# One layer of RWKV attention and a mixture of experts: all 36 expert pairs moved behind the last chunk, with the reciprocal in PSUM and eight late buffers

## The reference, cut to what matters

```python
x = x + attn(layernorm(x))      # 16 sequences of 256 tokens
x = x + moe(layernorm(x))       # 8 experts, top 2
# attn:
xn = ln(x); xp = shift(xn)
k, v = mix(xn, xp) @ Wk, mix(xn, xp) @ Wv;  r = sigmoid(mix(xn, xp) @ Wr)
a = ew * a + exp(k) * v;  b = ew * b + exp(k)      # a scan over the tokens
x = x + r * (a / (b + 1e-8)) @ Wo
yn = ln(x); kk = relu((0.5 * yn + 0.5 * shift(yn)) @ Wfk) ** 2
x = x + sigmoid(yn @ Wfr) * (kk @ Wfv)
# moe: scores = x @ gate.T; the 2 best experts of each token, softmax over the 2
y = sum of prob * ((silu(h1) * h2) @ w3[e]),  h1, h2 = x @ w12[e]
```

## Time and profile before

| what | value |
|---|---|
| median of 3 runs | 342.45 us |
| the profiled execution, its own time | 343.89 us |
| its span, first to last instruction | 342.2 us |
| PE busy | 267.1 us (78%) |
| DVE busy | 250.8 us (73%) |
| POOL busy | 213.2 us (62%) |
| ACT busy | 196.7 us (57%) |
| mean granted clock of TensorE, 1 being full | 0.902 |

### The profile page before, as it was taken

How to read it: one execution, slowest core, us unless ns; L and a number is a source line. 1 busy time by engine, 2 the same in 40 slices (tenths; PEclk the granted TensorE clock), 3 DMA queues, 4 the chain that set the end, 5 groups by cost and what they waited for, 6 DMA issues and landing times.

```text
span 342.2 us, 6282 instructions
## 1 busy us (share of the span) xinstructions
PE 267.1 (78%) x1684; PEld 210.0 (61%) x1684; DVE 250.8 (73%) x767; ACT 196.7 (57%) x412; POOL 213.2 (62%) x225
## 2 busy tenths in 40 slices
PE   0588599998969699794798799547999999989500
PEld 0234266665737357472587699436998999989400
DVE  3089998999799797999948657684466565565773
ACT  2546578887758738483496385323566665665100
POOL 5223457357857768578377775777777565665770
PEclk9999899999989969897699899856999999999855
DMA  7920000000101101011253111141522232232876
GB/s 265 445 66 1 0 0 33 1 34 23 40 31 42 54 23 41 32 42 54 65 129 106 39 51 61 39 118 49 131 72 82 79 92 81 81 83 73 269 262 228
DMA packets 22418, 29.23 MB, mean 85 GB/s; under 512 B 4317, under 2 KB 15583, under 8 KB 22128
## 3 DMA queue, kind: packets, MB, share of 16 engines
q1 hardware_dynamic: 14832, 13.45, 13.9%
q0 software_dynamic: 4352, 8.47, 7.4%
q10 hardware_dynamic: 3200, 6.90, 5.4%
HBM read 15.09 MB, written 12.14 MB: 80 GB/s over the span
## 4 chain that ended last, share of the span: by engine, by line
DVE 37%; PE 19%; issue 12%; POOL 9%; DMA 8%; ACT 2%; SPq 1%; DVEq 0%; POOLq 0%; ACTq 0%
PE p_up L831 10%; DVE rw L959 4%; DVE st L891 4%; DMA xg<-rows_d 3%; POOL res_d L449 3%; DMA res_d<-yo,xg 3%; DVE rden L952 3%; DVE gate_h L1121 2%; DVE num L946 2%; DVE den L942 2%; PE p_up L738 2%; PE p_f L750 2%; DVE xm L996 2%; POOL rows_d L431 2%; DVE mv L898 2%
## 5 line engine op out<-in xcount | busy, mean ns | idle before, releaser
L431 POOL DMA_INDIRECT rows_d<-rows,pos x64 | 66.4, 1037 | 23.6 <-issue 23.3
L831 PE MATMUL p_up<-xgT,w_up 128*128 128x128 f32 x576 | 74.4, 285 | 2.8 <-DVE hid L1125 2.8
L831 PEld LDWEIGHTS p_up<-xgT,w_up 128*128 128x128 f32 x576 | 71.3, 202 | 4.0 <-issue 3.4
L449 POOL DMA_INDIRECT res_d<-yo,xg x48 | 47.6, 991 | 26.2 <-issue 15.2
L1121 DVE SCALAR_TENSOR_TENSOR gate_h<-th,p_up 128x512 f32<-128x512 f32 x36 | 24.7, 687 | 41.5 <-ACT th L606 40.1
L626 ACT ACTIVATE w_up<-w_exp 128x512 f32 x72 | 41.4, 622 | 6.9 <-DVE slot_w L1105 4.6
L606 ACT ACTIVATE th<-p_up 128x512 f32<-128x512 f32 x36 | 21.4, 596 | 40.8 <-PE p_up L831 35.4
L738 PE MATMUL p_up<-ysum,w_sb 128*128 128x512 f32 x64 | 36.6, 675 | 2.9 <-POOL ysum L410 2.5
L750 PEld LDWEIGHTS p_f<-wfv_half,kk 128*128 128x128 f32 x256 | 31.1, 192 | 4.4 <-issue 3.5
L750 PE MATMUL p_f<-wfv_half,kk 128*128 128x128 f32 x256 | 32.7, 277 | 0.0
L449 POOL DMA_INDIRECT res_d<-o_raw x24 | 23.4, 974 | 9.9 <-issue 6.6
(11 more groups left out here) (169 smaller groups left out, 559.0 us busy)
## 6 DMA issues: line engine op xcount, KB each, us to landing
o_raw<-res_d SPq DMA_DIRECT2D x16, 256.0 KB, 5.2
xg<-rows_d SPq DMA_DIRECT2D x48, 65.0 KB, 2.0
w_exp<-experts ACTq DMA_DIRECT2D x1, 3072.0 KB, 16.8
x_all<-x SPq DMA_DIRECT2D x10, 256.0 KB, 2.3
out<-x_all ACTq DMA_DIRECT2D x8, 256.0 KB, 2.4
o_raw<-rows_d SPq DMA_DIRECT2D x24, 65.0 KB, 2.0
x_all<-x SPq DMA_DIRECT2D x1, 1536.0 KB, 16.6
rows_d<-rows,pos POOLq DMA_INDIRECT x64, 2.4
```

Source lines behind the costliest of these rows:

```text
L431: pool.indirect_dma_start(out=rows_d[:, :], out_offset=bass.IndirectOffsetOnAxis(ap=row, axis=0), in_=rows_of[is_last(c)][:, t, k, :], in_ ...
L449: pool.indirect_dma_start(out=res_d[:, :], out_offset=bass.IndirectOffsetOnAxis(ap=row, axis=0), in_=yo[b][:, n, :], in_offset=None, bound ...
L831: mm = pe.matmul(p_up[b][:, n, h * P:(h + 1) * P], w_up[q % 2][:, n, h * P:(h + 1) * P], xgT[q % 2][:, n, :], start=True, stop=True)
```

## The change

- No pair is woven into the pipeline on any engine. All 36 stand in `rest` behind the last chunk, alternate between the two bank pairs of PSUM from the first on, and the guards that kept woven pairs and chunks apart are empty. `early_shares`, five small DVE instructions, moves to iteration 10.
- `rden` is no tile of SBUF any more. It is the bank of `p_v`. So `v_in(c)` waits for `rw` of chunk c - 1 (it waited for `ekv` of that chunk), and `invert` waits for `ekv`.
- The rows and positions of even and odd chunks have a buffer each; chunk c waits for chunk c - 2.
- The late pairs have 8 buffers in 3 rounds (there were 6 in 4).
- Two early pairs share a semaphore for their loads.

```diff
-BUFS = 6
+BUFS = 8
-LAST_SINGLE = 6
+LAST_SINGLE = 0
-        rden = sb("rden", [P, CT]); gated = sb("gated", [P, CT]); rw = sb("rw", [P, CT])
+        gated = sb("gated", [P, CT]); rw = sb("rw", [P, CT])
+        rden = p_up[1][:, 1, :]
-            if c <= EARLY_CHUNKS:
-                after(eng, "dispatched_early", 16 * TPC * TOPK * c)
-            elif not is_last(c):
-                after(eng, "dispatched", 16 * TPC * TOPK * (c - EARLY_CHUNKS))
+            if c >= 2:
+                eng.wait_ge(dispatch_sem(c - 2), 16 * TPC * TOPK * ((c - 2) % EARLY_CHUNKS // 2 + 1))
-                loaded = S[f"early_loaded{q}" if q < EARLY_PAIRS else f"xg_loaded{b}"]
+                loaded = S[f"early_loaded{q // 2}" if q < EARLY_PAIRS else f"xg_loaded{b}"]
-                        row = pos_of[is_last(c)][:, k, t:t + 1]
+                        row = pos_of[c % 2][:, k, t:t + 1]
-            v_in = project(1, p_v, "v_done", lambda c: [("ekv_ready", c)])
+            v_in = project(1, p_v, "v_done", lambda c: [("rw_ready", c)])
 # invert
                 after(dve, "den_eps", c + 1)
+                after(dve, "ekv_ready", c + 1)
                 dve.reciprocal(rden[:, :], den[:, :]).then_inc(S["rden_ready"], 1)
 # up, pair 0
-                    pe.wait_ge(S["ekv_ready"], CHUNKS)
+                    pe.wait_ge(S["rw_ready"], CHUNKS)
 # POOL: the woven scatters of pairs 0 to 4 go
-            for q in range(5, PAIRS):
+            for q in range(0, PAIRS):
                 scatter(q)
 # ACT, PE, DVE: the woven tables become {} (DVE keeps {(10, 3): [(early_shares, 0)]})
-            rest([(turned_rows, -1), (tanh, 0), (expert_weights, -2)], (12, 8, 11))
+            rest([(turned_rows, -1), (tanh, 0), (expert_weights, -2)], (0, 0, 0))
-            rest([(turn_rows, -1), (up, 0), (down, 1)], (12, 9, 6))
+            rest([(turn_rows, -1), (up, 0), (down, 1)], (0, 0, 0))
-            rest([(gate_hidden, 0), (weigh, 1)], (7, 6))
+            rest([(gate_hidden, 0), (weigh, 1)], (0, 0))
```

More of the change, by code:

```diff
@@ L49 @@
 WHOLE = 8388608.0
[L50 to L54, removed]
+TURNED_AT = {}
+TURN_GUARDS = {}
+DOWN_AT = {}
+DOWN_GUARDS = {}
 NOWHERE = 2 * RESULTS
@@ L173, in build @@
         names += [f"{n}{b}" for n in ("xg_loaded", "scattered") for b in range(BUFS)]
-        names += [f"early_loaded{q}" for q in range(EARLY_PAIRS)]
+        names += [f"{n}{b}" for n in ("early_dispatched", "dispatched") for b in range(2)]
+        names += [f"early_loaded{n}" for n in range(EARLY_PAIRS // 2)]
         S = {n: sem(n) for n in names}
@@ L182, in V, with dispatch_sem @@
             return vec[:, VEC[n]:VEC[n] + 1]
-        def is_last(c):
-            return isinstance(c, int) and c == CHUNKS - 1
+        def dispatch_sem(c):
+            return S[f"early_dispatched{c % 2}" if c < EARLY_CHUNKS else f"dispatched{c % 2}"]
         def after_dispatched(eng, c):
-            if c <= EARLY_CHUNKS:
-                after(eng, "dispatched_early", 16 * TPC * TOPK * c)
-            elif not is_last(c):
-                after(eng, "dispatched", 16 * TPC * TOPK * (c - EARLY_CHUNKS))
+            if c >= 2:
+                eng.wait_ge(dispatch_sem(c - 2), 16 * TPC * TOPK * ((c - 2) % EARLY_CHUNKS // 2 + 1))
         def after(eng, name, count):
@@ L295, in load_early @@
                     sp.wait_ge(S["early_row"], 1)
-                    sp.wait_ge(S["dispatched_early"], 16 * EARLY_CHUNKS * TPC * TOPK)
+                    for c in (EARLY_CHUNKS - 2, EARLY_CHUNKS - 1):
+                        sp.wait_ge(dispatch_sem(c), 16 * TPC * TOPK * EARLY_CHUNKS // 2)
                 load(q)
@@ L304, in _ @@
             fill_pads(sp, range(E // 2))
-            sp.wait_ge(S["dispatched"], 16 * (CHUNKS - 1 - EARLY_CHUNKS) * TPC * TOPK)
-            sp.wait_ge(S["last_dispatched"], 16 * TPC * TOPK)
+            for c in (CHUNKS - 2, CHUNKS - 1):
+                sp.wait_ge(dispatch_sem(c), 16 * TPC * TOPK * (CHUNKS - EARLY_CHUNKS) // 2)
             sp.wait_ge(S["idle_filled"], 16)
@@ L427, in dispatch @@
                     for k in range(TOPK):
-                        row = pos_of[is_last(c)][:, k, t:t + 1]
+                        row = pos_of[c % 2][:, k, t:t + 1]
                         pool.indirect_dma_start(
                             out=rows_d[:, :], out_offset=bass.IndirectOffsetOnAxis(ap=row, axis=0),
-                            in_=rows_of[is_last(c)][:, t, k, :], in_offset=None, bounds_check=c + E * REGION, oob_is_err=False)\
-                            .then_inc(S["last_dispatched" if is_last(c) else
-                                        "dispatched_early" if c < EARLY_CHUNKS else "dispatched"], 16)
+                            in_=rows_of[c % 2][:, t, k, :], in_offset=None, bounds_check=c + E * REGION, oob_is_err=False)\
+                            .then_inc(dispatch_sem(c), 16)
             def dispatch_first(c):
@@ L591, in copy_rows @@
                 twice = xm[:, :, :].rearrange("p t (o d) -> p t o d", o=1).to_broadcast([P, TPC, TOPK, D])
-                act.activation(rows_of[is_last(c)][:, :, :, 0:D], twice, ACT.Copy).then_inc(S["rows_copied"], 1)
+                act.activation(rows_of[c % 2][:, :, :, 0:D], twice, ACT.Copy).then_inc(S["rows_copied"], 1)
             def gap_exp(c):
@@ L1048, in place @@
                 with nc.allow_low_precision(reason="whole numbers under 2**24, summed in float32"):
-                    dve.tensor_reduce(pos_of[is_last(c)][:, :, :], spots[:, :, :, :], mybir.AxisListType.X, ALU.add)\
+                    dve.tensor_reduce(pos_of[c % 2][:, :, :], spots[:, :, :, :], mybir.AxisListType.X, ALU.add)\
                         .then_inc(S["pos_ready"], 1)
@@ L1061, in label @@
                 after_dispatched(dve, c)
-                rows = rows_of[is_last(c)]
+                rows = rows_of[c % 2]
                 for k in range(TOPK):
@@ L1179, in _ @@
                            (late_table, 4)],
-                     {(8, 6): [(gate_hidden, 0)], (8, 8): [(weigh, 0)], (8, 9): [(gate_hidden, 1)],
-                      (9, 3): [(gate_hidden, 2), (weigh, 1)],
-                      (9, 5): [(early_shares, 0), (weigh, 2), (gate_hidden, 3), (weigh, 3), (gate_hidden, 4)],
-                      (10, 0): [(gate_hidden, 5), (weigh, 4), (gate_hidden, 6)], (10, 5): [(weigh, 5)]})
-            rest([(gate_hidden, 0), (weigh, 1)], (7, 6))
+                     {(10, 3): [(early_shares, 0)]})
+            rest([(gate_hidden, 0), (weigh, 1)], (0, 0))
             dve.wait_ge(S["x3_kept"], 16 * CHUNKS)
```

29 lines of the change are left out of this document (6 added, 23 removed).

## The result

The changed kernel takes 347.10 us (median of 4 runs, 346.59 to 347.74) against 342.51 us before (median of 4 runs on the same chip), a ratio of 1.0136 [1.0091, 1.0181] (in brackets the 95% interval): 1.4% slower. The forecast was 341.1 with a range of 336 to 346. The profiled execution took 346.91, its span is 345.1. The profiled one of before was 1.4 above its median, so the two spans differ by 2.9 where the medians differ by 4.6.

The account below looks back on a forecast made before the run. A DVE and POOL chain paces chunks, POOL the drain, PE the pairs. First `up` 212.0 + 2.0 + 101.5 puts the last at 315.5 (-1.4), tail unchanged: span 340.8, median 341.1 us, range 336.0 to 346.0.

Parts of the forecast that it names:

- The price of `rw`: DVE's `rw` with one PSUM input would take 0.69 us, not 3.95, freeing DVE 3.3 us sooner in three chunks.
- I take `spots` free at about +1.4, `seen` at +2.3 ... L417 at +4.1: 2.1 us a chunk, 6.3 in all.: Behind `rw`, each small DVE operation waits for one POOL operation; POOL's L417 starts 4.1 us after `rw`, gaining 6.3 in all.
- rival 2: Behind `rw`, `spots` waits for POOL's whole run of three; gain 2.3 us, not 6.3; 345.1, slower; chance 0.20.
- so 3.4 at worst. I take 2.7: Chunk 1: `v_in` waits for chunk 0's `rw`, costing 1.8 us, 3.4 with PE's lower clock; 2.7 taken, and it stays lost.
- `rw` of chunk 7: Last chunk's `rw`: -6.3 from shorter chunks and +2.7 from chunk 1 give -3.6 us, bounds -6.5 and +1.1.
- `full` keeps its 5.07: In the early table, `full` still waits 5.07 us for POOL's run of four; change 0.
- `v_in` waits at no cost from chunk 4 on: PE's `v_in` wait for the previous `rw` costs nothing, as PE has 3 us to spare; 2.4 a chunk without cover.
- The drain: Drain without pairs, set by POOL: L417 at 184.0 and 199.1, first `up` at 215.6, or 212.0 with the reciprocal's gain.
- part 1: Reciprocal in PSUM: shorter `rw` gains 6.3 us, chunk 1 costs 2.7; sum -3.6 at `rw` of chunk 7.
- Rival 3: One more wait of 3 to 4 us in the drain gives 344.5, slower; chance 0.13.
- The pairs: Pair stage: 35 `up` at 2.90 are 101.5 us, plus 2.0 for a low-clock start, no reload waits; last `up` 315.5.
- The tail "as before": Writing out, loading and adding behind the last `up` stays at 25.3 us.

Follow-up runs that it names:

- the added hole of 0.33 us: Changed kernel with one more wait on POOL: `shift_sum` waits until `spots` is through; 341.28 us, 0.9968.
- keeping the clock alone: Changed kernel with three unused 128x512 products on PE while it waits in chunk 1; 345.90 us, 1.0103.
- the woven kernel with the hole and the statistics first: Kernel before with eight buffers, PSUM reciprocal only in chunks 4 to 7, `ln3` statistics ahead of `spots`, `shift_sum` waiting for `spots`; 338.39 us, 0.9899.

## Why the prediction was wrong, step by step

**The price of `rw`** (0.69, from the row of `hid`): right, in all chunks.

**"I take `spots` free at about +1.4, `seen` at +2.3 ... L417 at +4.1: 2.1 us a chunk, 6.3 in all."** This is the step that failed. `spots` waited out the whole run, as rival 2 had it: L418 at +5.34, 0.84 a chunk, 2.5 in three. (Rival 2 gave 345.1, still 2.0 under the 347.1; it took the same 2.7 for chunk 1.) The prediction weighed the two kinds of rows and trusted, because it was the same instruction. Its reading of that row was right, but it was carried over to a run of another kind: POOL had been idle for 3.92 us ahead of L403 in chunk 3, while from chunk 4 on the run begins with an indirect DMA, and such a run kept DVE out in all 82 cases of the traces. The runs show that this wait was the cost: the added hole of 0.33 us made 0.53 of the 2.73 at the very place, and the kernel 5.8 us faster. What it is about the DMA stays open. The Trainium skill's page "SBUF — State Buffer", section "Who interferes with whom", says that whoever issues first has the shared pair of ports for the whole instruction and the other is blocked; the earlier trace rows and the 0.53 with a hole agree with a wait for one instruction, the 2.73 does not.

**"so 3.4 at worst. I take 2.7"** for chunk 1: it was 3.9. The mechanism was right, the size was off. The four products took 3.8 us: 1.85 at the full clock, not 1.72, and twice that, not 1.7 times, since all of them ran at 1.2 GHz. With 3.3 us won back by leaving this out for the early chunks, and 1.2 by keeping the clock alone, it is shown. That it "stays lost" was wrong in part: 0.8 of it had come back by chunk 3.

**`rw` of chunk 7**: forecast -3.6, measured 164.02 against 163.64, +0.4. Of the 3.9 us lost in chunk 1, 0.8 came back by `rw` of chunk 3 (76.11 against 73.02), 0.3 in chunk 3 and 2.4 in the three chunks behind it. The 4.0 us between forecast and measurement come from the two terms above, 3.8 of them from the first (2.5 won in three chunks in place of 6.3).

**`full` keeps its 5.07**: right (5.08). **`v_in` waits at no cost from chunk 4 on**: right; from POOL's `ln3_power` to the next `rw` it is 15.57 us (101.28 to 116.85) against 15.55 before (99.31 to 114.86), so the 0.84 won ahead of it is kept in full.

**The drain**: right. Without the gain of part 1 the forecast had L417 at 184.0 and 199.1 (184.25 and 199.23 measured), and the first `up` at 215.6, or 216.0 with the later `rw` (216.66 measured). Rival 3, a longer drain, did not come.

**The pairs**: right. 102.3 from first to last against 2.0 + 101.5, no wait for `xg`. Last `up`: 319.00, where the forecast with the +0.4 in place of -3.6 gives 319.5.

**The tail "as before"**: 26.1 against 25.3. In the 18 traces it lies between 25.1 and 26.7, so 0.8 is within what it varies by from kernel to kernel; no run was made for it.

**The whole**: on the span 345.1 against the forecast 340.8, 4.3 more, of which Part 1 is 4.0. In the medians it is 6.0, because the profiled execution of before lay 1.4 above its median and that of the changed kernel 0.2 below.

**What each part is worth**, by the runs: the order without woven pairs +7.6 (the prediction's own terms for it give about 6.8), the two more buffers -4 to -5, the reciprocal in PSUM 0 to +1.6. The sum is +2.6 to +5.2, and 4.6 was measured. The dispatch buffers by turns had no run of their own; from `rw` of chunk 0 to that of chunk 7 it is 134.8 us with them (the changed kernel in the woven order) and 134.6 without (the PSUM reciprocal alone), so the traces show no effect up to there. The changed kernel lost because the free `rw`, which with the buffers was to pay for the unweaving, handed its wait on, and because chunk 1 gave back the rest.

## What to carry to other kernels

When an instruction is freed from a wait for a resource, look which instruction stands behind it and needs the same resource: the wait goes there unless the resource comes free. A row that shows a short wait is evidence only together with what the other engine did in that moment and just before it: look for its idle time and for how its run of operations began before the price is taken over. A wait placed on the engine that holds a shared resource, where it costs 0.3 us, can be worth more than any instruction taken out.

## What the runs showed of the hardware

- A DVE instruction with two SBUF inputs, even one of 128x32 (and the one-input ones of the third point), that was issued while POOL was in a run that had begun with an indirect DMA waited on past the running operation, as a rule to the end of the run (2.73 us for the rest of three, 3.95 for three, 5.08 for four; 77 of 82 cases, the other five until one operation was left). 0.33 us in which POOL waited for a semaphore let it in (0.53), and cut `full` to 2.87.
- In a run that had begun after idle time and had no indirect DMA in it, it waited for the running operation alone, though the next followed without idle time (51 of 51 cases; 1.14 and 1.00 in the earlier trace rows, 1.01 in the woven kernel with the hole and the statistics first). What the DMA does to a run was not tried.
- `full` is such a case with a single tensor input of 128x8, and `var` waited too (0.83 and 0.92 in place of 0.17), so two tensor inputs are not the only condition. What the condition is for these one-input instructions was not tried.
- After 4.4 us without work on PE the next four 128x512 products ran at a granted clock of 0.50 and took 3.8 us instead of 1.8.
